# Pacing the gathers of a deformable convolution by their own landings in place of the gram

## What is computed

```python
# layer 0: x = x + deform(group_norm(x)); layer 1: x = x + zca_whiten(group_norm(x))
offsets = conv2d(x, offset_w, offset_b, 1)          # 3x3
mod = 1.0 + jnp.tanh(conv2d(x, mod_w, mod_b, 1))
kv = conv2d(x, kv_w, kv_b, 0)                       # 1x1
v = kv[:, C:].reshape(B, HEADS, HD, H, W)
px = xx + off[:, :, 0]; py = yy + off[:, :, 1]
sampled = bilinear(v, px, py) * mod                 # four corners per pixel and group
out = conv2d(sampled, out_w, out_b, 0)
# layer 1: covariance of 16 channels over all images (the gram), inverse root, apply
```

## Time and profile before

| | before |
|---|---|
| median of 3 runs | 6084.95 us (6083.93 to 6085.43) |
| span of the profiled execution | 7184.0 us (the page gives no other time of it) |
| GpSimd busy | 3896.8 us, 54% |
| VectorE busy | 4895.9 us, 68% |
| TensorE busy | 4541.9 us, 63%, mean granted clock 0.806 |
| gathers | 4096, first start 269.4, last 6483.4 us |
| DMA | 1600.64 MB, mean 223 GB/s |

### The profile page before, as it was taken

How to read it: one execution, slowest core, us unless ns; L and a number is a source line. 1 busy time by engine, 2 the same in 40 slices (tenths; PEclk the granted TensorE clock), 3 DMA queues, 4 the chain that set the end, 5 groups by cost and what they waited for, 6 DMA issues and landing times.

```text
span 7184.0 us, 65186 instructions
## 1 busy us (share of the span) xinstructions
PE 4541.9 (63%) x16382; PEld 2734.5 (38%) x16382; DVE 4895.9 (68%) x12991; ACT 957.1 (13%) x1820; POOL 3896.8 (54%) x4115
## 2 busy tenths in 40 slices
PE   6466666666566656666666656665667634337876
PEld 3234443343343434344344334433444423224332
DVE  7577776777677767777677767776767755546654
ACT  1111111111111111111111111111111101010000
POOL 0356666666566656666666656665666666660000
PEclk9778878787787878788788878877888867668999
DMA  6767765766576657677676757675666634446999
GB/s 216 251 209 223 229 227 190 228 222 218 191 226 220 218 183 229 224 224 224 196 224 218 225 184 228 216 224 179 205 205 204 194 121 136 139 137 264 427 427 410
DMA packets 896709, 1600.64 MB, mean 223 GB/s; under 512 B 80816, under 2 KB 605744, under 8 KB 862768
## 3 DMA queue, kind: packets, MB, share of 16 engines
q0 software_dynamic: 196608, 537.13, 23.3%
q10 hardware_dynamic: 579584, 536.90, 22.1%
q1 hardware_dynamic: 120368, 525.16, 21.3%
HBM read 1061.99 MB, written 536.87 MB: 223 GB/s over the span
## 4 chain that ended last, share of the span: by engine, by line
DVE 47%; another core or an unknown queue 22%; issue 15%; PE 7%; DMA 5%; ACT 2%; DVEq 1%; ACTq 1%; SPq 0%
DVE patch L683 10%; DVE psI L696 5%; DVE psI L698 5%; DVE psI L692 4%; DVE vring L566 4%; DMA out_dram<-patch 3%; DVE samp_mem L702 3%; DVE xr_mem L710 3%; DVE bst L489 2%; DVE taps L578 2%; ACT sampT L1290 1%; PE psO L1135 1%; ACTq L1380 1%; PE psA L1103 1%
## 5 line engine op out<-in xcount | busy, mean ns | idle before, releaser
L994 POOL DMA_INDIRECT patch<-v,index x4096 | 3890.8, 950 | 2584.5 <-issue 1531.4
L1103 PE MATMUL psA<-wB,xa_mem 128*128 128x364 f32 x3664 | 1420.1, 528 | 578.2 <-issue 423.8
L1135 PE MATMUL psO<-sampT,wO_sb 128*128 128x512 f32 x2048 | 1269.1, 770 | 106.8 <-issue 104.8
L1149 PE MATMUL psT<-ident,xr_mem 128*128 128x128 f32 x2048 | 445.4, 374 | 1312.0 <-DVE xr_mem L710 535.7
L1103 PEld LDWEIGHTS psA<-wB,xa_mem 128*128 128x128 f32 x3664 | 732.3, 211 | 1133.6 <-issue 699.9
L683 DVE TENSOR_TENSOR patch<-patch,psI 128x384 f32<-128x384 f32 x2048 | 1035.8, 547 | 61.6 <-issue 31.9
L1149 PEld LDWEIGHTS psT<-ident,xr_mem 128*128 128x128 f32 x2048 | 331.5, 192 | 1479.1 <-issue 917.3
L566 DVE TENSOR_TENSOR vring<-psA,biasB 128x256 f32<-128x256 f32 x956 | 398.9, 417 | 562.5 <-remote 504.8
L1135 PEld LDWEIGHTS psO<-sampT,wO_sb 128*128 128x128 f32 x2048 | 508.9, 262 | 698.1 <-issue 695.8
L702 DVE TENSOR_TENSOR samp_mem<-patch,psI 128x256 f32<-128x256 f32 x1024 | 430.6, 420 | 301.7 <-ACT sampT L1290 162.5
L1273 ACT ACTIVATE vring<-vring 128x512 f32<-128x512 f32 x512 | 321.0, 627 | 2364.2 <-DVE vring L566 1516.4
(11 more groups left out here) (227 smaller groups left out, 2989.0 us busy)
## 6 DMA issues: line engine op xcount, KB each, us to landing
v<-vring ACTq DMA_DIRECT2D x128, 2048.0 KB
xr_mem<-x_dram SPq DMA_DIRECT2D x130, 1024.0 KB
xa_mem<-x_dram SPq DMA_DIRECT2D x128, 1024.0 KB, 7.1
x<-xr_mem ACTq DMA_DIRECT2D x128, 1024.0 KB
xs_mem<-x_dram SPq DMA_DIRECT2D x101, 1024.0 KB, 8.9
patch<-v,index POOLq DMA_INDIRECT x4096
patch<-x SPq DMA_DIRECT2D x64, 1024.0 KB, 10.4
out_dram<-patch ACTq DMA_DIRECT2D x64, 1024.0 KB, 49.4
```

The costliest lines, as they stand in the source:

```text
L994: eng.indirect_dma_start(out=patch[n][:, t, :], out_offset=None, in_=v2_flat[k], in_offset=bass.IndirectOffsetOnAxis(ap=index[:, at:at + 1 ...
L1103: mm = eng.matmul(conv_bank[wide][r][:, 0:NA], row, wB[:, c, :], start=(c == 0), stop=(c == CC - 1))
L1135: mm = eng.matmul(psO[o][:, :], wO_sb[:, h, o * P:(o + 1) * P], sampT[:, h, :], start=(h == 0), stop=(h == CC - 1))
L1149: mm = eng.transpose(psT[h][:, at:at + P], xr[m][j][:, c, row * W:(row + 1) * W], ident[:, :])
```

## The change

The wait for the gram before the ninth gather goes. Instead GpSimd waits before every fourth gather, through the new function `landed`, until the four gathers two fours back have landed; for the first two fours of a block these are the last two fours of the block before (none at an image's start). So no more than eight gathers are on their way at a time, except around an image's start. Each buffer has four landing semaphores in place of two, each for four gathers, and VectorE waits for one before each part u in place of one before each half.

```diff
+FOUR = 4
-        got = [[sem(f"got{n}{h}") for h in range(2)] for n in range(RING)]
+        got = [[sem(f"got{n}{f}") for f in range(NJ // FOUR)] for n in range(RING)]
...
-                eng.wait_ge(got[n][h], (b * (PAIRS // 2) + q) * (NH * 16) + NH * 16)
...
                 for u in range(2):
                     t = u * (NH // 2)
+                    eng.wait_ge(got[n][2 * h + u], (b * (PAIRS // 2) + q) * (FOUR * 16) + FOUR * 16)
...
+            def landed(b, i, j, four):
+
+                if four < 0:
+                    if j == 0 and i == 0:
+                        return
+                    i, j, four = i - 1 + j, 1 - j, four + NJ // FOUR
+                n = 2 * (i % 2) + j
+                eng.wait_ge(got[n][four], (b * (PAIRS // 2) + i // 2) * (FOUR * 16) + FOUR * 16)
...
-                    if t == NH:
-
-                        eng.wait_ge(psG_full[j], b * PAIRS + i + GRAM_FULL - 2)
+                    if t % FOUR == 0:
+                        landed(b, i, j, t // FOUR - 2)
                         alone(eng)
...
-                    ).then_inc(got[n][t // NH], 16)
+                    ).then_inc(got[n][t // FOUR], 16)
```

## The result

The changed kernel takes 6259.33 us (median of 4 runs, 6251.99 to 6266.54). The kernel before took 6085.19 us beside it (4 runs, 6083.93 to 6091.98). The ratio is 1.0285, with a 95% interval of 1.0273 to 1.0297: 2.9% slower, 174 us. The forecast of 6095 us and its range to 6145 both missed. The profiled execution of the changed kernel took 6266.54 us itself, with a span of 6264.8 us, so this profile can be read straight against the timed runs.

What follows compares the result with a forecast made beforehand. GpSimd's gathers, issued nearly without pause, were taken to bound the timed run. From 6085 us: 0 for the gram wait, +13 for late landings, 0 for wait instructions, -3 for finer semaphores, giving 6095 us; 8-in-10 range 6040 to 6145.

Steps and rivals of the forecast that it cites:

- The root: GpSimd's gather step, 1.254 us, bounds the timed run; a time change above 1% either way would refute it.
- rival B: Faster: timed gather step under 1.254 us and gram wait real, so removing it gains; 6015 to 6070 us, chance 0.20.
- Part (1): GpSimd's wait for psG_full, before each block's ninth gather, goes 256 times; saving in the timed run taken as 0.
- Part (2): Landing waits added before every four gathers cost nothing if a landing takes no longer than the 5.45 us cover.
- Part (3): Landing times bounded from pauses: unloaded 1.7 to 2.7 us; loaded at most 4.6, 5.4 to 5.9, and 5.1 us.
- Part (4): Cost of late landings at GpSimd's waits: 512 loaded fours at 0.025 us each, 13 us.
- x: Average lateness of a landing beyond the cover, over the loaded fours: taken as 0.05 us.
- the halving for "a lasting lateness": Since every landing wait looks two fours back, a lasting lateness x costs only x/2 per four.
- Part (5): The added wait instructions, three more a block on GpSimd and two on VectorE, cost 0.
- Part (6): Finer semaphores let VectorE start on a block's first four before the second has landed: gain 3 us, once.
- A: Slower: landing waits hold GpSimd while loads and stores run, mean loaded landing 5.5 us; 6110 to 6150 us, chance 0.30.
- C: Slower: without the gram wait, streaming gathers hold up TensorE's results in timed runs too; 6150 to 6215 us, chance 0.07.

Runs made afterwards that it cites:

- e0: The kernel before, unchanged, run once more for its profiled execution: 6092.34 us, span 6090.6 us.
- e7: The kernel before with the last of each block's 16 gathers left out and VectorE's semaphore counts lowered to match: 5794.34 us, ratio 0.9522.
- e1: The kernel before without GpSimd's wait for TensorE's gram and nothing in its place: 6083.99 us, ratio 0.9996.
- e4: The changed kernel with each landing wait looking one four back, not two: 9313.09 us (one run).
- e2: The changed kernel without its landing waits, the four semaphores a block kept: 6084.47 us, ratio 1.0001.
- e3: The changed kernel with each landing wait looking three fours back, not two: 6085.24 us, ratio 1.0002.
- e6: The changed kernel with the landing wait only before the last four of a block, 256 waits of 1024: 6170.25 us, ratio 1.0144.
- e5: The changed kernel with the gram wait put back beside the landing waits: 6265.10 us, ratio 1.0302.

## Why the prediction was wrong

**The root held.** GpSimd's gathers bound the timed run. e0 shows them end to end, and e7 gives 292 us for 256 of them. The prediction read this from a disturbed profile by summing the steps, and the inference that the profile's pauses weren't in the timed run is confirmed. The 48 us by which that sum was too high were mostly the 27.8 us of the earlier trace rows (absent in e0), 5135 - 5129.8 = 5 us for a step of 1.253, and 700.6 - 690.8 = 10 us behind the last gather. The rest lies within the spread of the runs. They weren't a shorter step, as rival B would have it.

**Part (1), the gram wait at 0:** right, by e1.

**Part (2), a cover of 5.45 us:** right. In the changed kernel 0.79 us pass from the semaphore to the held start, where 0.8 was taken from the earlier trace rows.

**Part (3), the landing times, is the step that failed.** The prediction says "All traffic was down by then, so the landings took at most 4.6, 5.4 to 5.9, and 5.1 us". Two things were wrong with it, and both made the bounds too short. First, the traffic wasn't down. The shares of 0.11 and 0.10 in the earlier trace rows are not zero, and the windows after them still show transfers (kernel before, first profile, columns as in the earlier trace rows):

```profile
3000.50:3001.00 0.50, 0.47 (x2) 0.47 (x3) 0.49 (x2) 0.00 (x0) 0.16 (x1) 0.50 0.06 25
3001.00:3001.50 0.50, 0.50 (x5) 0.50 (x4) 0.50 (x2) 0.00 (x0) 0.50 (x1) 0.50 0.02 8
...
3048.50:3049.00 0.50, 0.50 (x5) 0.50 (x4) 0.50 (x2) 0.00 (x0) 0.50 (x1) 0.50 0.02 8
```

The gathers that ended the pauses, at 3000.84 and 3048.35, can't have made these: in the trace their first packets come 1.65 us after their starts, and the last of the old ones ends at 3001.2 and 3048.7. Second, the end of the traffic isn't the landing; the semaphore comes later, in e4 by 0.34 us. The trace holds the semaphores' events themselves. The last ones of the halves that the three gathers close come 5.71, 5.71 and 5.78 us after the gathers' starts. This profile has only 12414 of the 65536 events, so these are lower bounds. All three lay over the cover of 5.45 us, by 0.26 us and more, where the prediction saw two clear of it. The words "at most" should have been "at least".

The longest landings lie still further out. The view of the gathers' landings (us) for e2 and for the changed kernel, of which only the longest is used here, since the middle one depends on which landings could be tied to one gather:

```profile
DMA to landing us min/median/max: 2.6/5.2/7.7
```

```profile
DMA to landing us min/median/max: 2.6/2.8/8.0
```

Single gathers thus took up to 7.7 and 8.0 us. By the semaphores' events the slowest four of e2 landed 8.4 us after its last gather's start, still under e3's cover of 10.5 us (nine steps less 0.79).

The estimate of 2.3 us from the Trainium skill's figures ("DMA: Bandwidth & Descriptors", section "Anatomy of one DMA - SWDGE (gpsimd) path") is near e4's unloaded 2.62 and less than half of its loaded 5.97. The prediction was right not to use it for loaded landings, but its own bounds still lay too close to it.

**Part (4), the size of the lateness:** wrong with it, in both factors. x was put at 0.05 us over 512 loaded fours. By e2's semaphore events and a release of 0.79 us, 316 fours are late, by 204 us in all. Over the 512 that is 0.40 us, eight times as much. And the halving for "a lasting lateness" doesn't hold. When every hold delays all that comes after it, as in the replay, 175 of the 204 us are left and not 102, and e6 shows the same at one position: late fours mostly stand apart, and each is paid nearly in full. The measured loss is 174 us; the formula as written would have given 102 even with the right x. The sentence that a held gather "keeps itself out of the queue that made it late" was no reason for a small x: the holds took 172 us all the same.

**Part (5), the wait instructions at 0:** right, by e3, which has all but eight of them. **Part (6), a gain of 3 us:** not seen; e2 stands at 1.0001, and its interval of 0.1% to either side, 6 us, is too wide to rule it out.

**The rivals.** A named the mechanism, the place and the mean landing, with 0.30, but took its price from the same three rows: 26 to 64 us. Its upper end used the same "at most" that failed in part (3), and the same halving as part (4); nothing else in it was wrong. B and C fell in e1, C once more in e5.

**What the profile was to show.** The gram row is gone and the step stays 0.95 + 0.30, as forecast. The test for A, more than a few dozen pieces or one of 2 us, was sharp enough: there are 189, and the list of waits has them up to 3.2 us.

```profile
POOL patch L1003 <- DMA patch<-v,index: 189.8, 189, 3.2
```

Wrong was the profiled span of about 7180 us. It is 6264.8, because the slow execution of the earlier trace rows didn't repeat in any later profile, the one of the kernel before among them. Wrong too was that GpSimd's idle would lie at block starts on VectorE's sampling: L703 has 0.3 us.

## What to carry to other kernels

A wait on the bounding engine was free here only with a cover beyond the longest landing under full traffic, and the price is steep at the edge: nine starts of cover cost nothing, six 22 us, five 174, four 571. Price such a wait from many landings while everything runs, the longest ones above all, counted to the semaphore. A DMA share that has fallen to 0.1 is not the end of a transfer, and the last packet is not the landing. And where a profile's span is 18% over the timed runs, argue from the timed ones, or profile once more, before any duration of a transfer is taken from it.

## What the runs showed that was not expected

- One profiled execution of the kernel before was 18% longer (7184.0 us) than its runs, with TensorE's results reaching other engines late. The repeat had 6090.6 us and none of it. The first profile also holds only 12414 of the 65536 events of the gathers' semaphores, the repeat 65412. What disturbed the first one stays open; nothing in the comparisons depends on it.
- Doubling the x1 stores, 134 MB more in the loop, changed the time without landing waits by nothing (0.9999, interval 0.9990 to 1.0009).
- From a landing on the semaphore to the start of the gather behind it 0.79 us passed (0.02 + 0.02 + 0.76 in the chain), against 0.30 us between two gathers without a hold.
- A gather of 131 KB landed after 2.62 us with only its own four beside it and after 5.97 us under loads that filled the DMA engines (e4). Of the 2.62 us, 1.64 pass before its first packet starts and 0.34 after its last one ends.
